# A decoder layer in float32 on one core: POOL's three normalisations add a negated mean where they subtracted the mean

## What is computed

```python
x = _layernorm(x + _L0_attn_ref(x, ...))        # in-projection, convolution of 4 taps, SiLU, a scan over 16 states
x = _layernorm(x + _L0_xattn_ref(ctx, x, ...))  # 8 heads of 128; keys and values from the latents and the context
x = _layernorm(x + _L0_ffn_ref(x, ...))         # 8 experts, 2 for each token, a capacity for each expert

def _layernorm(x, axis=-1, eps=1e-05):
    m = jnp.mean(x, axis=axis, keepdims=True)
    v = jnp.var(x, axis=axis, keepdims=True)
    return (x - m) / jnp.sqrt(v + eps)
```

## Time and profile before

| What | Value |
|---|---|
| Time, median of 3 runs | 1028.47 us (1027.39 to 1030.19) |
| Span of the profiled execution | 1025.7 us |
| Instructions | 21471 |
| Busy: PE, DVE, ACT, POOL | 979.9, 809.4, 729.3, 568.7 us |
| Granted TensorE clock, mean | 0.984 |

### The profile page before, as it was taken

The page is one execution under the profiler, slowest core; times in us unless marked ns, Lnnn a source line. Parts: engine busy times, 40 slices in busy tenths (PEclk is TensorE's granted clock), DMA queues, the critical chain, the costliest instruction groups (busy, mean ns, idle before and its releaser), DMA issues.

```text
span 1025.7 us, 21471 instructions
## 1 busy us (share of the span) xinstructions
PE 979.9 (96%) x7018; PEld 929.5 (91%) x7018; DVE 809.4 (79%) x2040; ACT 729.3 (71%) x1865; POOL 568.7 (55%) x967
## 2 busy tenths in 40 slices
PE   8999999999999999999999999999999999999960
PEld 7799999999999999999999999999999999899960
DVE  6887878887888888888888888878887877655526
ACT  6686868787777777776877787868786766365536
POOL 4743464656566556554656566545656463526543
PEclk9999999999999999999999999999999999999985
DMA  7643031213111311113110311041105110386448
GB/s 248 220 135 110 6 118 36 61 35 108 47 50 46 101 53 51 45 59 96 51 45 30 125 51 46 17 137 50 47 11 171 33 41 11 140 293 126 67 60 315
DMA packets 63829, 89.60 MB, mean 87 GB/s; under 512 B 14932, under 2 KB 44680, under 8 KB 63720
## 3 DMA queue, kind: packets, MB, share of 16 engines
q1 hardware_dynamic: 56040, 75.51, 22.8%
q0 software_dynamic: 7680, 12.72, 5.8%
HBM read 49.21 MB, written 38.99 MB: 86 GB/s over the span
## 4 chain that ended last, share of the span: by engine, by line
PE 77%; ACT 8%; DVE 6%; issue 3%; DMA 3%; POOL 1%; SPq 0%; ACTq 0%; DVEq 0%; POOLq 0%
PE ps L611 20%; PE ps L612 20%; PE ps L613 20%; PE ps L640 7%; PE ps L719 3%; DVE nmx L1800 2%; DMA accd<-yo,tku 1%; ACT fx L1378 1%; PE ps L655 1%; PE ps L757 1%; PE ps L657 1%; POOL accd L2174 1%; ACT hp L1076 1%; ACT ys_x L1179 1%; ACT prob L1237 1%
## 5 line engine op out<-in xcount | busy, mean ns | idle before, releaser
L2085 POOL TENSOR_SCALAR prob<-prob,rinv 128x333 f32<-128x333 f32 x256 | 144.4, 575 | 242.1 <-DVE rinv L1809 241.1
L1232 ACT ACTIVATE oT_hi<-ps 128x256 fp32r<-128x256 f32 x126 | 48.5, 385 | 151.4 <-PE ps L657 151.4
L611 PE MATMUL ps<-kv_lo,w_hi 128*128 128x256 f32 (+1 forms) x512 | 154.4, 302 | 1.1 <-DVE kv_lo L1386 1.1
L613 PE MATMUL ps<-kv_hi,w_hi 128*128 128x256 f32 (+1 forms) x512 | 153.4, 300 | 0.0
L612 PE MATMUL ps<-kv_hi,w_lo 128*128 128x256 f32 (+1 forms) x512 | 153.1, 299 | 0.0
L1237 ACT ACTIVATE prob<-ps,nmx 128x333 f32<-128x333 f32 x256 | 135.0, 538 | 7.4 <-DVE nmx L1800 7.4
L1386 DVE TENSOR_TENSOR pT_lo<-ps,pT_hi 128x512 fp32r<-128x512 f32 x254 | 131.8, 550 | 1.1 <-ACT pT_hi L1249 0.3
L1800 DVE TENSOR_REDUCE nmx<-ps 128x2 f32<-128x666 f32 x128 | 108.3, 846 | 9.3 <-PE ps L613 7.9
L640 PE MATMUL ps<-ident,prob 128*128 128x128 f32 (+1 forms) x768 | 105.5, 272 | 1.8 <-POOL prob L2085 1.0
L611 PEld LDWEIGHTS ps<-kv_lo,w_hi 128*128 128x128 f32 x512 | 96.9, 189 | 1.6 <-issue 1.5
L612 PEld LDWEIGHTS ps<-kv_hi,w_lo 128*128 128x128 f32 x512 | 96.5, 189 | 0.0
(11 more groups left out here) (308 smaller groups left out, 3284.6 us busy)
## 6 DMA issues: line engine op xcount, KB each, us to landing
wraw<-in_W SPq DMA_DIRECT2D x14, 512.0 KB, 7.9
vcd_hi<-vst_hi SPq DMA_DIRECT2D x10, 512.0 KB, 2.7
vcd_lo<-vst_lo SPq DMA_DIRECT2D x10, 512.0 KB, 3.5
v_hi<-vcd_hi SPq DMA_DIRECT2D x32, 154.0 KB
v_lo<-vcd_hi SPq DMA_DIRECT2D x32, 154.0 KB
slots<-initr SPq DMA_DIRECT2D x8, 520.0 KB, 7.8
xs<-in_x SPq DMA_DIRECT2D x16, 256.0 KB, 4.4
xts<-in_xT SPq DMA_DIRECT2D x15, 256.0 KB, 4.1
```

The source lines that it names most:

```text
L611: pe.matmul(dst, hi1, lo2, start=first, stop=False, skip_group_check=True)
L613: return pe.matmul(dst, hi1, hi2, start=False, stop=last, skip_group_check=True)
L2085: pool.tensor_scalar(prob[:, h % 2, t, 0:KEYS], prob[:, h % 2, t, 0:KEYS], rinv[:, h % 2, t:t + 1], 1.0, ALU.mult, ALU.mult).then_inc(norm ...
```

## The change

DVE writes the negated means into a new tile nm of 3x2 float32 numbers a partition: one instruction more in each of the steps `context_stats`, `mixed` and `residual_stats`, behind the same wait as the variance instruction that follows it and covered by that one's semaphore. On POOL the three normalisations read the negated mean and add it, and then multiply as before. DVE's own normalisations (lnp, xrow_b) and the last layer norm stay as they were.

```diff
         a_vv = s1("a_vv", [P, 2, NT])
+        nm = s1("nm", [P, 3, NT])
+        a_nm, c_nm, x_nm = [nm[:, i, :] for i in range(3)]
         a_rs = s1("a_rs", [P, 2, NT])
...
                 need(dve, xstat_set, 3 * c + 2)
+                dve.tensor_scalar(x_nm[:, 0:1], x_mv[:, 0:1], -1.0, None, ALU.mult)
                 dve.tensor_scalar(x_vv[:], x_mv[:, 1:2], EPS, None, ALU.add).then_inc(xstat_set, 1)
...
+                dve.tensor_scalar(a_nm, a_mv[:, :, 0], -1.0, None, ALU.mult)
                 dve.tensor_scalar(a_vv[:, 0, :], a_mv[:, :, 1], 1.0, EPS, ALU.mult, ALU.add).then_inc(astat_set, 1)
...
                 need(dve, cstat_set, 5 * b - 1)
+                dve.tensor_scalar(c_nm, c_mv[:, :, 0], -1.0, None, ALU.mult)
                 dve.tensor_scalar(c_vv[:], c_mv[:, :, 1], EPS, None, ALU.add).then_inc(cstat_set, 1)
...
-                pool.tensor_scalar(cxn[:], cxs[:], x_mv[:, 0:1], x_rs[:], ALU.subtract,
+                pool.tensor_scalar(cxn[:], cxs[:], x_nm[:, 0:1], x_rs[:], ALU.add,
                                    ALU.mult).then_inc(cxn_set, 1)
...
-                    pool.tensor_scalar(x1[1 - par][:, t, :], xa[:, t, :], a_mv[:, t, 0:1],
-                                       a_rs[:, 0, t:t + 1], ALU.subtract, ALU.mult).then_inc(x1p_set, 1)
+                    pool.tensor_scalar(x1[1 - par][:, t, :], xa[:, t, :], a_nm[:, t:t + 1],
+                                       a_rs[:, 0, t:t + 1], ALU.add, ALU.mult).then_inc(x1p_set, 1)
...
-                            pool.tensor_scalar(xrow[:, t, 0:D], xb[:, t, :], c_mv[:, t, 0:1], c_rs[:, t:t + 1],
-                                               ALU.subtract, ALU.mult).then_inc(x2_set, 1)
+                            pool.tensor_scalar(xrow[:, t, 0:D], xb[:, t, :], c_nm[:, t:t + 1], c_rs[:, t:t + 1],
+                                               ALU.add, ALU.mult).then_inc(x2_set, 1)
```

## The result

Over five runs each, on one chip, the changed kernel has a median of 1032.55 us (1032.26 to 1034.04) and the kernel before of 1027.39 us (1027.35 to 1030.19). The ratio is 1.0047, with a 95% interval of 1.0035 to 1.0059: about 5 us slower. The forecast was 1029.0 with a range up to 1030.9; it stood on a median of 1028.47 for the kernel before, and as a step it was +0.5 us. The profiled execution spans 1030.8 us, against 1025.7 before, at a granted clock of 0.986 against 0.984, so the trace holds the whole loss and the clock explains none of it.

A forecast was written before the change was run, and what follows sets the result against it. TensorE was taken to bound the kernel, busy 979.9 of 1025.7 us. With POOL's price unchanged and addresses at 0, DVE's negations added 0.48 us: span 1026.2, time 1029.0 us, range 1026.7 to 1030.9.

The forecast's parts named there:

- The price on POOL (a): POOL's 72 normalisations: adding then multiplying was taken to cost the same 1.22 us each as subtracting.
- lower bound of 465 ns: POOL's changed normalisation at 256 columns if quick, worked out from L2085 and L2149; a saving of 0.75 us each.
- rival (1): Addition is quick on POOL, relief hidden except at first cxn and den; -0.14 us, time 1028.3 us, chance 0.38.
- estimate of 384 ns: POOL normalisation of 256 columns, at 1.5 ns an element for the best one-input loop, plus a fixed part.
- Where a quicker POOL arrives (b): Quicker POOL reaches the chain only at first cxn (0.15 us) and den at 822.23 (0.39 us); steady loop 0.
- two gains granted in this step: If POOL is quicker: 0.15 us at DVE's wait for a context tile at 15.68, 0.39 us at k_lo, 824.12.
- The negations (c): 42 added DVE instructions, 0.08 us each, at most 0.17; hidden in the steady loop, 0.48 us on the chain.
- Six places: Where the chain passes DVE's variance instruction, at 6.51, 16.36, 26.05, 40.97, 69.35 and 884.02 us; 0.48 us, at most 1.0.
- The address of the tile (d): The new tile nm takes 24 bytes a partition and moves the tiles behind it; price taken as 0.
- Rival (2): Faster: POOL's 54 us do reach TensorE's idle time from 60 to 890 us; 1022.2 at best, chance 0.06.
- Rival (3): Slower: POOL shuts out the new DVE instructions, 0.24 us for each of 15 c_nm; time 1032.6 us, chance 0.06.
- the sign to look for: Steady loop: two-batch period changing by over 0.3 us, or TensorE waiting for DVE or POOL, would refute the forecast.

The follow-up runs named there:

- third kernel of part 1: The changed kernel with x1 subtracting as before, while cxn and xrow are made by additions; 1030.16 us, ratio 1.0021 against the kernel before.
- control of part 3: The kernel before with the cast of idxf and the mask moved behind oT_lo on DVE; 1027.68 us, ratio 1.0004.

## Why the prediction was wrong, point by point

**The price on POOL (a).** Taken at 1.22 us, measured at 549 ns. The reading of L2137 failed: that an addition in front which is 46 ns dearer than a multiplication puts the form in the slow class. Those 46 ns at 2 columns don't grow with the columns into 0.67 us: at 256 columns the form with an addition in front is 84 ns over the 465 ns worked out for a multiplication, and only the one that subtracts is slow. The sentence "subtraction as such isn't slow in the two-tensor form" was right and beside the point. Why POOL takes so long there isn't shown; the pointer changes tile together with the operation (a_nm for a_mv), and no run parts the two. The lower bound of 465 ns was 84 ns too low; its slope was taken between two instructions with different operations. The rival (1), which had the right class, would have forecast 1028.3 us, and so this step alone isn't what put the time out of the range. The estimate of 384 ns and a fixed part for 256 columns, worked out from the Trainium skill (GPSIMD Engine Reference, Performance versus the Vector engine), is nearer to the measured 549 ns than to the subtraction's 1219.

**Where a quicker POOL arrives (b).** This is the step that failed and put the time out of the range: the prediction's "Where a quicker POOL would arrive" took the relief in the steady loop at 0, and it cost 4.5 us. Its sentences "With L2012 quicker, L2016 is over before den starts" and "In the steady loop the same collision costs TensorE nothing" carry a whole-kernel conclusion on den's behalf alone. The instruction that blocks is not the one that was made quicker, it is the next one, of unchanged length (1.28 us), and it moved by 1.34 us. I asked what it leaves; I didn't ask what it lands on. The rows to ask it of were one view away: DVE's timeline of the 1.3 us ahead of den, with idxf, mask and oT_lo in it, and the only slack between them and TensorE the 0.21 us of idle time before oT_lo. A block of 0.75 us (0.62 at the cast, 0.13 at the mask) less 0.28 of slack and overlap makes oT_lo 0.47 us late, of which the period shows 0.4; in the three late batches with a context tile oT_lo is 0.70 us late, and the period shows 0.7. Six times 0.4 and three times 0.7 are 4.5 of the loop's 4.95 us; the step of 0.36 is most of the rest. The two gains granted in this step: den's mean did fall, from 712 to 439 ns, but the 0.39 us at 824.12 didn't become a gain, since the last batch paid its own block at the cast instead (0.70 us at 826.96); from the last L721 to that k_lo matmul it is 19.41 us against 19.51. The 0.15 us of cxn can be seen in the third kernel of part 1 alone. In the changed kernel the load was issued 0.61 us sooner (8.12 against 8.73), took 7.83 us instead of 6.92, and landed 0.30 later.

**The negations (c).** 0.08 us a place was right (16.65 and 16.72 are the starts of x_nm and x_vv), and none was blocked. Six places were to cost 0.48 us, of which five lie ahead of 113 us; at 58 us the changed kernel is 0.51 late, but 0.30 of that is the later landing of the context tile, and with the tile alone, without any negation, it is 0.32 late, with all 42 and the quick cxn of part 1 0.05 early. So the term is borne out in kind, and its sum is lost in the scatter of the beginning. The "0" for the loop was wrong by the one step of 0.36 us.

**The address of the tile (d).** 0 was forecast; 0.3 us is what the trace shows, unmeasurable in the time.

**The rivals.** Rival (2), a gain, is excluded: TensorE's waits had not named POOL, and relieving POOL gained nothing even with the side effect removed. Rival (3) named the right obstacle, a DVE instruction held until one of POOL's ends, and the wrong instructions: it looked for victims among the instructions that were added, not among those already there. Its 1032.6 us agrees with the 1032.55 measured by accident. What it drew on is borne out: the Trainium skill (SBUF — State Buffer, Who interferes with whom) describes the ports which DVE and POOL share as an exclusive lock, and here cast, mask and den each end within 0.05 us of the end of the POOL instruction beside them (292.99 and 292.97; 559.60 and 559.55; 293.19 and 293.16). One row doesn't fit a lock for the whole instruction: in the kernel before, the mask at 555.65 is lengthened to 0.52 us and ends 0.62 us ahead of the second x1 beside it (556.17 and 556.79). "I am wrong if the loop's period of two batches changes by over 0.3 us, if TensorE shows a wait for DVE or POOL inside it" was the sign to look for, and it came.

**The chances.** 0.06 for slower was too little for an argument in which the relieved engine shares a resource with the one ahead of TensorE, and in which the price of the changed instruction was open by a factor of 2.6. The 0.38 given to the quick form ought to have been split by where the cvec addition then falls.

## What to carry to other kernels

An instruction that becomes quicker moves everything queued behind it. If one of these blocks a resource of another engine, slide it along that engine's timeline by the time saved and name every instruction that it now covers, with the slack each has before the bounding engine waits. Short instructions that only prepare later work, here a cast of 4 columns and a mask of 32, are safer behind the one that the bounding engine waits for than ahead of it: moving them there took the changed kernel from a ratio of 1.0047 to 1.0008. And the relief of an engine that no wait of the bounding engine named was worth nothing here, so that its side effects were all there was.

## What the runs showed of the hardware

With two pointers per partition and 128x256 float32, POOL takes 1219 ns to subtract and then multiply and 549 ns to add and then multiply (the pointer's tile differs between the two). A negated operand from DVE costs 0.07 to 0.08 us there (16.65 to 16.72).

A DVE instruction of 0.16 us (128x4, uint32 to float32), one of 0.19 us (128x32) and one of 0.16 us (128x2) can each last 1.2 to 1.3 us if POOL's 1.28 us addition of two tensors begins just before them (cast 1.21 at 292.08 in the control of part 3, mask 1.32 at 558.28, den 1.20 at 291.99 before). DVE's oT_lo, which reads 128x256 numbers of PSUM and as many of SBUF, keeps its 0.42 us with the same addition around it (131.46 in the changed kernel with the victims moved). Who wins is decided by hundredths of a microsecond: at 558 us the addition came 0.01 us ahead of mask and the batch lost 0.7 us, and at 131 us both started at the same hundredth and mask took its usual 0.19.
